# Layers 2 and 3 of attention: one PSUM bank for each kind of product, score banks that change places, and all turned tiles at the end of a cycle

## The reference

```python
def _L3_xattn_ref(hidden_states, encoder_hidden_states, Wq, Wk, Wv, Wo, bo):
    ...
    q = hidden_states @ Wq
    k = encoder_hidden_states @ Wk
    v = encoder_hidden_states @ Wv
    ...
    scores = jnp.einsum('bhsd,bhkd->bhsk', q, k) * scale
    probs = jax.nn.softmax(scores, axis=-1)
    out = jnp.einsum('bhsk,bhkd->bhsd', probs, v)
    out = out.transpose(0, 2, 1, 3).reshape(B, S, H * Dh)
    out = out @ Wo + bo
    return out
...
    x = x + _L3_xattn_ref(_layernorm(x, axis=-1), ctx_768, L3_xattn_Wq, L3_xattn_Wk, L3_xattn_Wv, L3_xattn_Wo, L3_xattn_bo)
```

## Time and profile before

| | |
|---|---|
| median of 3 runs | 1448.45 us (1447.54 to 1449.8) |
| span of the profiled execution | 1450.7 us |
| PE busy | 1374.7 us, 95% |
| PEld busy | 1008.5 us, 70% |
| DVE busy | 1000.6 us, 69% |
| ACT busy | 945.3 us, 65% |
| POOL busy | 743.7 us, 51% |
| attention of layer 2 | 522.2 to about 784 us of the span |
| attention of layer 3 | 918.9 to about 1430 us of the span |

### The profile page before, as it was taken

How to read it: one execution, slowest core, us unless ns; L and a number is a source line. 1 busy time by engine, 2 the same in 40 slices (tenths; PEclk the granted TensorE clock), 3 DMA queues, 4 the chain that set the end, 5 groups by cost and what they waited for, 6 DMA issues and landing times. The chain is left out here.

```text
span 1450.7 us, 30070 instructions
## 1 busy us (share of the span) xinstructions
PE 1374.7 (95%) x9799; PEld 1008.5 (70%) x9799; DVE 1000.6 (69%) x2375; ACT 945.3 (65%) x1951; POOL 743.7 (51%) x763
## 2 busy tenths in 40 slices
PE   7999989998998989999998998999999999999998
PEld 5555548897665867777775777677777777777766
DVE  6877846677657667777776566576767767677683
ACT  4787776775666556666664465576766667676663
POOL 5455641111752146666655576465656556565642
PEclk9999999999999999999999999899999999999999
DMA  6300000000001300000001000000000000000002
GB/s 172 82 0 0 1 15 16 1 1 1 1 1 48 88 0 2 2 0 0 0 0 37 1 0 2 0 1 1 1 0 0 0 0 0 0 0 0 1 6 83
DMA packets 31517, 20.57 MB, mean 14 GB/s; under 512 B 9569, under 2 KB 29000, under 8 KB 31432
## 3 DMA queue, kind: packets, MB, share of 16 engines
q1 hardware_dynamic: 31204, 19.38, 4.8%
q10 hardware_dynamic: 228, 0.10, 0.0%
HBM read 18.42 MB, written 1.05 MB: 13 GB/s over the span
## 5 line engine op out<-in xcount | busy, mean ns | idle before, releaser
L2354 POOL TENSOR_TENSOR arena<-arena,l3a_rinv 128x512 f32<-128x512 f32 x256 | 258.9, 1040 | 205.8 <-DVE l3a_rinv L2735 205.4
L2631 ACT ACTIVATE arena<-l3a_scores_ps,l3a_nmax 128x512 f32<-128x512 f32 x256 | 174.7, 685 | 118.5 <-DVE l3a_nmax L2729 118.5
L2354 POOL TENSOR_TENSOR arena<-arena,l2a_rinv 128x512 f32<-128x512 f32 x128 | 129.4, 1040 | 96.1 <-DVE l2a_rinv L2735 95.2
L2729 DVE TENSOR_REDUCE l3a_nmax<-l3a_scores_ps 128x2 f32<-128x1024 f32 x128 | 156.0, 1219 | 19.5 <-PE l3a_scores_ps L2427 19.4
L874 ACT ACTIVATE l0a_prob<-l0a_scores_ps,l0a_k_scale 128x1024 f32<-128x1024 f32 x128 | 135.5, 1112 | 35.2 <-PE l0a_scores_ps L724 34.5
L2440 PE MATMUL l3a_turned_ps<-const,arena 128*128 128x128 f32 x1024 | 144.7, 274 | 3.0 <-DVE l3a_probT L2741 1.6
L2741 DVE COPY l3a_probT<-l3a_turned_ps 128x512 f32<-128x512 f32 x128 | 88.5, 691 | 80.6 <-PE l3a_turned_ps L2440 80.4
L2440 PEld LDWEIGHTS l3a_turned_ps<-const,arena 128*128 128x128 f32 x1024 | 119.3, 141 | 26.1 <-issue 8.5
L2451 PE MATMUL l3a_work_ps<-l3a_probT,l3a_v 128*64 128x256 f32 x1024 | 125.3, 387 | 2.3 <-DVE x_tokens L2756 1.6
L2631 ACT ACTIVATE arena<-l2a_scores_ps,l2a_nmax 128x512 f32<-128x512 f32 x128 | 87.4, 686 | 56.4 <-DVE l2a_nmax L2729 56.4
L2451 PEld LDWEIGHTS l3a_work_ps<-l3a_probT,l3a_v 128*64 128x64 f32 x1024 | 69.4, 137 | 52.8 <-issue 24.0
(11 more groups left out here) (768 smaller groups left out, 3609.4 us busy)
## 6 DMA issues: line engine op xcount, KB each, us to landing
l1f_w<-in_L_ffn_w SPq DMA_DIRECT2D x16, 256.0 KB, 2.7
arena<-in_ctx SPq DMA_DIRECT2D x4, 384.0 KB, 5.4
w_l_w<-in_L_ffn_W SPq DMA_DIRECT2D x1, 1024.0 KB
arena<-in_L_ffn_W SPq DMA_DIRECT2D x16, 64.0 KB, 1.8
out_x<-x_tokens SPq DMA_DIRECT2D x8, 128.0 KB, 1.9
x_tokens<-in_x SPq DMA_DIRECT2D x1, 896.0 KB, 7.5
const<-in_constants SPq DMA_DIRECT2D x1, 525.0 KB
w_l_wo<-in_L_xattn_Wo SPq DMA_DIRECT2D x1, 512.0 KB
```

Of the source, the lines that this page charges most:

```text
L2354: e.tensor_tensor(prob[n][:, :], prob[n][:, :], bcast(rinv[:, n:n + 1], [P, S]), ALU.mult).then_inc(m.prob_ready, 1)
L2631: e.activation(prob[at][:, :], bank(u), ACT.Exp, bias=nmax[:, at:at + 1], accum_out=rsum[:, at:at + 1]).then_inc(m.exp_ready, 1)
L2729: e.tensor_reduce(nmax[:, at:at + 2], sps[:, i * 1024:(i + 1) * 1024].rearrange("p (h k) -> p h k", h=2), AX.X, ALU.max, negate=True).then ...
```

## The change

- Banks by kind: Q and y in `tps[0]`; K, z's tiles, late tiles in `tps[1]`; V in `work[1]`; weighted values in `work[0]`.
- The four turned tiles of a cycle go to four banks: units 0 and 1 to the banks of scores 0 and 1 of the running cycle, whose exponentials have been taken; units 2 and 3 to `work[0]` and `work[1]`.
- The scores of the next cycle therefore begin in the two banks that hold no turned tile: in odd cycles units 0 and 1 are in banks 2 and 3, units 2 and 3 in banks 0 and 1 (`place`).
- PE's order in a cycle: scores; join at c == 2; weighted; z's tiles at c == 3; V; Q; K; turned 0, 1, 2, 3. In the first batch's cycle 3, K comes behind the turned tiles.
- Waits: scores' first half waits for all exponentials of the cycle before, the second half for the copies of turned tiles 0 and 1. Turned 0 and 1 wait for exponentials 0 and 1 of the running cycle, 2 for the copy of the weighted values, 3 for the copy of V. `x_updated` is waited for before Q, no longer before weighted. K waits for the low part of the K before it, no longer for V's copy.
- ScalarE's order: K's copy directly behind Q's, then the copies of turned tiles 1 and 3 (before: tile 1, Q, K, tile 3). VectorE's order in the loops stays.
- The last batch and the experts take other banks to fit; the last tiles use bank 0 and `work[1]` in turn.

No instruction that computes is added or removed in the loops.

```diff
         def slot(c, u):
             return c % 2 * UNITS + u
+
+
+
+        def place(b, c, u):
+            return u if c % 2 == 0 or (is_first(b) and c == 1) else (u + 2) % UNITS
+
+        def scores_bank(b, c, u):
+            return bank(place(b, c, u))
+
+        def turned_bank(b, c, u):
+            return scores_bank(b, c, u) if u < 2 else work[u - 2]
+
+        def last_turned_bank(u):
+            return work[1] if u % 2 else bank(0)
 
...
                 wait(e, m.q_lo_ready, n)
-                wait(e, m.o_kept, n - 2 * AHEAD + 1)
-                e.matmul(work[0][:, 0:T], wq_hi[:, pair], z_hi[:, tokens], start=True, stop=False)
-                e.matmul(work[0][:, 0:T], wq_lo[:, pair], z_hi[:, tokens], start=False, stop=False)
-                e.matmul(work[0][:, 0:T], wq_hi[:, pair], z_lo[:, tokens], start=False, stop=True).then_inc(m.q_projected, 1)
+                e.matmul(tps[0][:, 0:T], wq_hi[:, pair], z_hi[:, tokens], start=True, stop=False)
...
             def project_k(b, c, side):
                 n = C * b + c
                 pair = slice(c * P, (c + 1) * P)
-                if isinstance(n, int) and n < AHEAD:
-                    wait(e, m.k_lo_ready, n)
-                else:
-                    e.wait_ge(m.v_kept, n + 1)
+                wait(e, m.k_lo_ready, n)
                 if c == 0:
                     e.wait_ge(m.c_lo_ready, b + 1)
-                e.matmul(work[1][:, :], wk_hi[:, pair], c_hi[side % SIDES][:, :], start=True, stop=False)
-                e.matmul(work[1][:, :], wk_lo[:, pair], c_hi[side % SIDES][:, :], start=False, stop=False)
-                e.matmul(work[1][:, :], wk_hi[:, pair], c_lo[side % SIDES][:, :], start=False, stop=True).then_inc(m.k_projected, 1)
+                e.matmul(tps[1][:, :], wk_hi[:, pair], c_hi[side % SIDES][:, :], start=True, stop=False)
...
                 for i in halves:
                     queries = slice(i * P, (i + 1) * P)
-                    wait(e, m.exp_ready, UNITS * (n - 1) + 2 * i + 2)
+                    if is_first(b) and c == 1:
+                        e.wait_ge(m.exp_ready, 2 * i + 2)
+                    elif i == (0 if is_first(b) and c == 2 else 1):
+
+                        wait(e, m.pT_kept_dve, 2 * n - 3)
+                        wait(e, m.pT_kept_act, 2 * n - 3)
+                    else:
+                        wait(e, m.exp_ready, UNITS * n)
                     for k, (q, key) in enumerate(((q_hi, k_hi), (q_hi, k_lo), (q_lo, k_hi))):
                         for h in range(2):
                             rows = slice(HD * h, HD * h + HD)
-                            last = e.matmul(bank(2 * i + h), q[c % 2][rows, queries], key[c % 2][rows, :], start=k == 0, stop=k == 2,
-                                            tile_position=(HD * h, 0))
+                            last = e.matmul(scores_bank(b, c, 2 * i + h), q[c % 2][rows, queries], key[c % 2][rows, :], start=k == 0,
+                                            stop=k == 2, tile_position=(HD * h, 0))
                     last.then_inc(m.scores_ready, 1)
 
-            def turned(b, c, u):
+            def turned(b, c, u, out):
                 n = C * b + c
                 e.wait_ge(m.prob_ready, UNITS * n + u + 1)
-                wait(e, m.pT_kept_act if u % 2 else m.pT_kept_dve, 2 * n + u // 2)
-                if is_first(b) and c == 0 and u < AHEAD:
-                    e.wait_ge(m.v_kept, u + 1)
-                if u == 0 and c == 2:
-                    e.wait_ge(late.z_lo_ready, 1) if is_first(b) else e.wait_ge(ahead.z_kept, b)
                 for t in range(KT):
-                    last = e.transpose(tps[u % 2][:, t * P:(t + 1) * P], prob[slot(c, u)][:, t * P:(t + 1) * P], g.ident)
+                    last = e.transpose(out[:, t * P:(t + 1) * P], prob[slot(c, u)][:, t * P:(t + 1) * P], g.ident)
                 last.then_inc(m.turned, 1)
+
+            def turned_in_cycle(b, c, turn_c, more, u):
+                n = C * b + c
+                if u < 2:
+                    e.wait_ge(m.exp_ready, UNITS * n + u + 1)
+                elif is_first(b) and c == 1:
+                    e.wait_ge(m.v_kept, u)
+                elif u == 2:
+                    e.wait_ge(m.o_kept, n - 1)
+                else:
+                    e.wait_ge(m.v_kept, n + 3 if c + AHEAD < C or more else C * B)
+                turned(*turn_c, u, turned_bank(b, c, u))
 
...
             def turn_finished(b, n):
-                e.wait_ge(m.pT_kept_dve, 2 * n)
+                e.wait_ge(m.k_lo_ready, n + 3)
                 if isinstance(b, int) and b < 0:
-                    late.tensor(e, 0, tps[0])
+                    late.tensor(e, 0, tps[1])
                 else:
-                    ahead.tensor(e, b, tps[0])
+                    ahead.tensor(e, b, tps[1])
 
...
+                    choosing = experts and not more
+                    if c == 0 and first:
                         scores(b, c)
-                    if c == 0 and first:
                         project_q(0, 1, 0)
                         project_k(0, 1, 0)
-                        project_v(0, 0, 0, tps[0])
+                        project_v(0, 0, 0)
                         keep_warm(8)
                         continue
                     if c == 1 and first:
+                        scores(b, c, range(1))
+                        project_v(0, 1, 0, work[0])
+                        scores(b, c, range(1, TPB))
+                        e.wait_ge(m.v_kept, 1)
                         project_v(0, 2, 0)
-                        turned(0, 0, 0)
                         project_q(0, 2, 0)
-                        turned(0, 0, 1)
                         project_k(0, 2, 0)
-                        turned(0, 0, 2)
-                        turned(0, 0, 3)
+                        for u in range(UNITS):
+                            turned_in_cycle(b, c, turn_c, more, u)
                         project_q(0, 3, 0)
-                        project_v(0, 3, 0)
+                        e.wait_ge(m.k_lo_ready, 3)
+                        project_v(0, 3, 0, tps[1])
                         continue
+                    scores(b, c)
                     if c == 2 and first:
+                        e.wait_ge(m.v_kept, 4)
                         project_k(0, 3, 0)
                     if c == 2 and not first:
+                        e.wait_ge(m.q_lo_ready, n + 2 if c + 1 < C or more else C * B)
+                        for i in range(TPB):
+                            last = join(b - 1, i, tps[0][:, i * P:(i + 1) * P], range(C))
+                        last.then_inc(m.y_ready, 1)
+                    weighted(*back)
+                    if c == 3:
+                        if onward:
+                            turn_finished(b - 1, n - 1)
+                        else:
+                            e.wait_ge(m.k_lo_ready, C * B)
+                            ahead.tensor(e, b - 1, tps[1])
+                    if choosing and c == 4:
                         e.wait_ge(m.q_lo_ready, n + 2)
-                        for i in range(TPB):
-                            last = join(b - 1, i, work[0][:, i * P:(i + 1) * P], range(C))
-                        last.then_inc(m.y_ready, 1)
-                        if onward:
-                            project_v(*on)
-                        e.wait_ge(m.x_updated, TPB * b)
-                    if c >= 2 or not first:
-                        if c + 1 < C or more:
-                            e.wait_ge(m.q_lo_ready, n + 2)
-                        weighted(*back)
-                    if c == 3:
-                        turn_finished(b - 1, n - 1)
-                    choosing = experts and not more
-                    if choosing and c == 4:
                         experts.early.tensor_scores(e, tps[0], g.zT[:, 0:(B - 1) * T:T])
-                    if onward and not (c == 2 and not first):
+                    if onward:
                         project_v(*on)
-                    if choosing and c == 4:
-                        e.wait_ge(experts.early.scores_taken, 1)
+                        if choosing and c == 4:
+                            e.wait_ge(experts.early.scores_taken, 1)
+                        if c == 2 and not first:
+                            e.wait_ge(m.x_updated, TPB * b)
+                        project_q(*on)
+                        if c == 3 and not first:
+                            e.wait_ge(ahead.z_kept, b)
+                        if not (c == 3 and first):
+                            project_k(*on)
                     closing = c == C - 1 and not more
                     if closing:
-                        if experts:
-                            e.wait_ge(experts.early.index_ready, 1)
-                            e.wait_ge(experts.early.chosen_ready, 1)
                         join_last(0, range(0, C - 3))
-                    if turns_here:
-                        turned(*turn_c, 0)
-                    if onward:
```

(28 more changed lines are left out.)

114 lines of the change are left out of this document (60 added, 54 removed).

## The result

| | kernel before | changed kernel |
|---|---|---|
| median, first comparison | 1449.12 us (4 runs) | 1435.74 us (4 runs), ratio 0.9909, 95% interval 0.989 to 0.9929 |
| median, second comparison | 1448.34 us (22 runs) | 1437.09 us (6 runs), ratio 0.9926, 95% interval 0.9904 to 0.9949 |
| span of the profiled execution | 1450.7 us | 1436.4 us (its time 1438.69 us) |
| a looped batch of layer 2, of layer 3 | 31.83, 62.28 us | 31.12, 61.52 us |

What follows compares the result with a forecast made beforehand. TensorE was taken to set the time, so only PE's losses could be won. 9.1 + 2.2 + 1.6 - 0.2 = 12.7 us took the median from 1448.45 to 1435.8 us; 8-in-10 range 1431 to 1445.5.

Steps and rivals of the forecast that it cites:

- step 5: Looped batches: losses of 0.90 and 0.82 us go, less 0.1 kept per batch; 9.1 us won, from 4.1 to 10.3.
- The cause named first: Behind the join, weighted values wait for VectorE to take y from the same bank: 0.42 and 0.27 us idle PE.
- the small rest: Looped batches: third tile waits for first's copy, loop's branch behind that, Q waits for weighted values' copy; called small.
- The loss of 0.1 us per batch to longer lists of waits: Looped batches: 0.1 us per batch kept as lost to loop register arithmetic and the longer wait list before scores.
- bare work: PE's cost of a looped batch with nothing late: 30.93 us in layer 2, 61.46 us in layer 3.
- step 4: Next scores' waits: VectorE slack 0.2 us, ScalarE's tile 1 copy 0.4, tile 3 copy 0.8; price nothing.
- rival C: ScalarE's tile 1 copy bounds scores' second half every cycle, losing about 0.3 us each: 1464.6 us; chance 0.10.
- step 1: Own banks, new PE order: plain cycle stays 7.16 us; bounds -0.17 to +0.12 us a cycle, taken as nothing.
- rival D: Clock falls while 16 tiles' matmuls run in a row, 163 us more: about 1599 us; chance 0.01.
- step 6: First batches, cycles 2 and 3: 1.1 us won per layer, 2.2 together, between 0.8 and 3.2.
- step 7: End of layer 2: waits of 0.84 and 0.73 us go; 1.6 us won, from 0.5 to 2.5.
- step 8: End of layer 3: choice chain starts 0.7 us later, 0.4 to 0.7 given back; loss 0.2, between +0.8 and -1.5.

Runs made afterwards that it cites:

- the pair with real and met waits: Changed kernel with tiles between projections, plus waits of tiles 2, 3 for copies of tiles 0, 1: real 1449.38 us; count two lower, already met, 1431.64 us.
- VectorE in good order: Changed kernel with VectorE's second reciprocal of a cycle ahead of tile 0's copy: 1429.38 us, ratio 0.9862 to the kernel before.
- The search kernel: Changed kernel with the search for the largest score ahead of tile 0's copy in layer 3's last batch, cycle 4: 1434.16 us, ratio 0.9887.

## Why the prediction was right, step by step

**Looped batches (step 5): 8.35 us won, 9.1 forecast.** From the start of the second batch to that of the last, layer 2 became 3.94 us shorter (190.73 to 186.79) and layer 3 4.41 (373.61 to 369.20). By cycles that is 7.8 with the join, 1.6 in plain cycles and 1.0 at the edge of layer 3's loop, less 2.1 lost in cycle 3. The cause named first, the join's wait behind a shared bank, is shown by putting it back: 5.0. The other 2.8 of the join's cycle fits Q's wait for the copy of the weighted values, which the forecast named as one of the small rest; it is read from the trace and not isolated. That the plain cycles and the edge lost to waits on the shared banks of tiles, with the loop's branch and arithmetic behind them, is what the pair with real and met waits speaks for, though there they cost some four times as much in a plain cycle as in the kernel before. The loss of 0.1 us per batch to longer lists of waits was not there: a batch of layer 3 with VectorE in good order takes 61.19, under the 61.46 taken for its bare work. That term was too high: z's cycle costs 0.20 more than a plain one of 7.15, not 0.25 and 0.15 for a change of shape.

**What step 4 missed.** It followed VectorE's copies and found 0.2 us of slack, and asked nothing about POOL, which starts behind the reciprocal that the step itself put behind tile 0's copy. That cost 0.33 us in 12 batches, 4.0 us, and is why a batch took 61.52 and not 61.19. The forecast of the batches came near because two errors met: the bare work was put too high, and this loss was not seen.

**ScalarE's copy (step 4, rival C).** Forecast: ends 0.1 to 0.2 us into the cycle, harmless until about 0.5. Measured in plain cycles: 0.10; nothing lost at 0.3, 0.00 to 0.03 at 0.53; and 0.30 at 0.84 in the cycle behind z's (the forecast said 0.3 at 0.85). Both halves were right, and with them the small chance given to C.

**Own banks (step 1).** Q and K fell to 0.35 and 0.70, as forecast for a place without a tile ahead of them, and the four tiles rose from 1.69 to 1.84 of the possible 1.98. The sum moved by 0.04 at most. Tiles between the projections give 7.16, so the place is free on PE.

**The clock (rival D).** The granted clock is 1.00, the level of 2.4 GHz, in a cycle with 16 matmuls of tiles in a row. The Trainium skill, TensorE: Matmul & The Clock Gate, Part 4: PE-mode transpose, has it that such work does not bring the full clock on. The forecast's rival made of it that the clock would fall, and this trace does not agree with that: 1.84 us of such work in each 7.15 us, between matmuls of other kinds, leaves it at 1.00. What transposes do alone, no run here shows.

**First batches (step 6): 1.0 us won, 2.2 forecast.** Without their first cycle they won 1.21 (layer 2) and 1.40 us (layer 3), a little above the forecast. The first cycle took much of it back: 7.24 for 6.20 and 5.96 for 5.35. The granted clock in it was 0.82 and 0.89 in the changed kernel, and in a variant with the same code in this cycle it was 1.00 and the cycle took 6.04 and 5.35. So this loss comes and goes from run to run; the wait at the earlier trace rows itself is gone, and one of 0.78 us at the late tiles in front of it has come (0.70 in layer 2), which the forecast did not have.

**End of layer 2 (step 7): 1.6 forecast.** The three cycles that can be compared win 1.30, all in the join's (8.88 to 7.58). From there to layer 3 another 0.74 us was won, but this stretch took 147.3 to 152.9 us in kernels with hardly any difference in it, so that figure says nothing.

**End of layer 3 (step 8): 0.5 won, 0.2 lost forecast.** The mechanism was right, the chain of the choice started late behind tile 0's copy, but both terms were too small: cycles 4 to 6 lost 1.5 us (24.50 to 25.96) where 0.7 was said, and what follows cycle 6 won 2.0 (41.2 to 39.2) where 0.4 to 0.7 was said. The search kernel shows that 2.3 us lay in cycles 5 and 6.

**The sum.** 8.35 + 1.0 + 2.0 + 0.5 = 11.8 us in the stretches of the change (with the 0.74 behind layer 2), against 12.7. The second comparison's 11.25 is near that. The medians of the first differ by 13.4, and its two traces by 14.3, of which 2.5 lie ahead of the changed code. So that the first median meets the forecast to 0.1 us is luck; right is the size, and the causes named for most of it.

## What to carry to other kernels

When one engine is full, look at what each move does to the engine that waits two steps behind the moved one: here a copy in front of a reciprocal moved POOL's scaling onto VectorE's normalization. A wait that is met just in time is not free in a hardware loop: what the sequencer has queued behind it is no longer hidden. And read a forecast's gain by stretch, since runs of unchanged code moved by more than some of its terms.

## What the runs showed of the hardware

VectorE's normalization, which reads and writes SBUF, does not finish while POOL's scaling runs. It took 0.33 to 0.37 us alone or when a scaling had 0.28 us or less to go; with POOL at work for longer it took up to 1.15 in the looped batches, and then ended 0.08 us behind one of POOL's operations. VectorE's copy out of PSUM took its 0.69 us beside the same scaling (the row at 1055.48). The Trainium skill, SBUF — State Buffer, section SBUF: two separate sides, gives a reason: in some of its operations VectorE needs a pair of ports that it shares with GpSimd, and the one that starts first holds them for a whole instruction. The times agree with it; that it is these ports, no run here shows. The forecast should have used it, all the more as its own trace had it, in layer 2's last batch of the kernel before, where two operations take 0.91 and 1.11 us that take 0.17 and 0.6 with POOL idle:

```profile
764.39 0.91 DVE L262 TENSOR_SCALAR l2a_ahead_var_eps<-l2a_ahead_mean_var 128x2 f32<-128x2 f32 x1
...
768.28 1.11 DVE L272 TENSOR_SCALAR l2a_ahead_z<-x_tokens,l2a_ahead_mean_var,l2a_ahead_rstd 128x128 f32<-128x128 f32 x2
```

Tiny operations of the search pay as well; in the changed kernel's last batch, DVE and POOL:

```profile
1378.24 1.06 DVE L2094 TENSOR_SCALAR l3a_early_w<-l3a_early_w,l3a_early_red 7x8 f32<-7x8 f32 x1
1379.33 0.96 DVE L2095 TENSOR_TENSOR l3a_early_w<-l3a_early_w,const 7x8 f32<-7x8 f32 x1
```

```profile
1378.24 2.04 POOL L2368 TENSOR_TENSOR arena<-arena,l3a_rinv 128x512 f32<-128x512 f32 x2 [0.52 <-DVE l3a_rinv L2767]
```

Operations on 56 elements take as long as one scaling of 128x512, twice in a row; the first of them took 0.28 us in the kernel before. Copies on ScalarE overlap: eight of 64 columns, 1.05 us together, start 0.10 us apart.
